# Summing the denominators of two pairs of key tiles in one visit instead of two

## What is computed

```python
q = (x1 @ wq.T).reshape(b, n, HEADS, HEAD_DIM).transpose(0, 2, 1, 3)
k = (x2 @ wk.T).reshape(b, m, HEADS, HEAD_DIM).transpose(0, 2, 1, 3)
v = (x2 @ wv.T).reshape(b, m, HEADS, HEAD_DIM).transpose(0, 2, 1, 3)
dots = jnp.einsum('bhnd,bhmd->bhnm', q, k) * SCALE
attn = jax.nn.softmax(dots, axis=-1)
out = jnp.einsum('bhnm,bhmd->bhnd', attn, v)
```

## Time and profile before

| | us |
|---|---|
| median of 3 runs | 1866.66 |
| lowest and highest | 1865.8, 1867.45 |
| the profiled execution | 1869.96 |
| its span, first to last instruction | 1867.9 |
| TensorE matmul busy | 1843.9 |
| VectorE busy | 1256.4 |
| ScalarE busy | 878.9 |
| GpSimd busy | 850.0 |
| VectorE: maxima (L1758), 1024 | 626.2 |
| VectorE: transposes of denominators (L1780), 78 | 55.6 |
| TensorE: denominators (L1448) | 98.7 |

### The profile page before, as it was taken

One profiled execution on the slowest core, in us unless ns is written; L12 is line 12 of the kernel. 1 busy time (PEld: TensorE's weight loads), 2 busy tenths in 40 slices (PEclk: granted clock), 3 DMA queues, 4 the chain that ended last, 5 costly groups with the idle time before them and its releaser, 6 DMA issues.

```text
span 1867.9 us, 27863 instructions
## 1 busy us (share of the span) xinstructions
PE 1843.9 (99%) x10488; PEld 1290.6 (69%) x10488; DVE 1256.4 (67%) x2339; ACT 878.9 (47%) x1587; POOL 850.0 (46%) x822
## 2 busy tenths in 40 slices
PE   9999999999999999999999999999999999999998
PEld 7786688788655555555555554554469998899986
DVE  6675574278787888888798799778554444344457
ACT  4322323322665666666465465457624443344433
POOL 4002201100598999998677577676122223222232
PEclk9999999999999999999999999999999999999999
DMA  8003535684767586858554443451244454534544
GB/s 289 24 1 118 186 103 178 199 243 144 170 139 168 130 202 130 176 112 178 109 135 114 103 118 87 112 115 63 79 148 127 132 142 107 141 91 131 145 111 155
DMA packets 124502, 250.19 MB, mean 134 GB/s; under 512 B 11312, under 2 KB 29504, under 8 KB 119680
## 3 DMA queue, kind: packets, MB, share of 16 engines
q1 hardware_dynamic: 109696, 187.56, 34.3%
q0 software_dynamic: 14672, 60.85, 16.0%
HBM read 148.46 MB, written 62.42 MB: 113 GB/s over the span
## 4 chain that ended last, share of the span: by engine, by line
PE 86%; DVE 9%; DMA 2%; issue 1%; POOL 1%; SPq 0%; ACT 0%; DVEq 0%; POOLq 0%; ACTq 0%
PE banks L1225 35%; PE banks L1540 12%; PE banks L1413 11%; PE banks L1424 11%; PE banks L1394 10%; DVE max L1758 5%; PE banks L1448 4%; PE banks L1231 2%; DMA raw<-in_x_t 1%; DVE den_t L1780 1%; PE banks L1325 1%; DMA k_half<-in_xwk_t 0%; DMA k_stack<-k_parts 0%; POOL x_nat L2297 0%; DVE hot_row L1936 0%
## 5 line engine op out<-in xcount | busy, mean ns | idle before, releaser
L2286 POOL TENSOR_TENSOR probs<-probs,probs 128x512 f32<-128x512 f32 x464 | 584.8, 1305 | 194.1 <-PE banks L1424 193.1
L2164 ACT ACTIVATE probs<-banks 128x512 f32<-128x512 f32 x1024 | 517.6, 626 | 286.9 <-PE banks L1413 286.4
L1758 DVE TENSOR_REDUCE max<-banks 128x1 f32<-128x512 f32 x1024 | 626.2, 680 | 37.4 <-PE banks L1394 37.0
L1413 PE MATMUL banks<-q_stack,k_stack 98*128 98x512 f32 x1024 | 403.3, 407 | 0.1
L1394 PE MATMUL banks<-k_stack,q_stack 98*128 98x512 f32 x1024 | 400.1, 398 | 1.4 <-DVE den_t L1780 1.1
L1413 PEld LDWEIGHTS banks<-q_stack,k_stack 98*128 98x128 f32 x1024 | 191.0, 187 | 151.7 <-issue 101.1
L1424 PE MATMUL banks<-probs,v_grp 128*32 128x512 f32 x2048 | 252.3, 605 | 0.0
L1394 PEld LDWEIGHTS banks<-k_stack,q_stack 98*128 98x128 f32 x1024 | 192.6, 188 | 48.5 <-DVE max L1758 13.5
L2344 POOL DMA_INDIRECT y_rows<-eo,tok x35 | 69.8, 1994 | 172.3 <-DVE eo L1991 116.2
L1424 PEld LDWEIGHTS banks<-probs,v_grp 128*32 128x32 f32 x2048 | 60.3, 110 | 118.3 <-issue 112.0
L1978 DVE TENSOR_TENSOR hid_lo<-hid,hid_hi 128x640 fp32r<-128x640 f32 x64 | 52.8, 824 | 126.3 <-ACT hid_hi L2233 126.3
(11 more groups left out here) (273 smaller groups left out, 2795.8 us busy)
## 6 DMA issues: line engine op xcount, KB each, us to landing
k_stack<-k_parts SPq DMA_DIRECT2D x144, 256.0 KB, 5.4
probs<-probs POOLq DMA_DIRECT2D x36, 1024.0 KB, 10.1
w_raw<-in_L_ffn_w SPq DMA_DIRECT2D x16, 2048.0 KB, 8.4
q_stack<-q_parts SPq DMA_DIRECT2D x48, 256.0 KB
v_grp<-v_rows SPq DMA_DIRECT2D x48, 256.0 KB, 3.5
raw<-in_ctx_t SPq DMA_DIRECT2D x8, 1024.0 KB, 6.6
k_parts<-out_hi SPq DMA_DIRECT2D x32, 256.0 KB, 2.5
k_parts<-out_lo SPq DMA_DIRECT2D x32, 256.0 KB, 3.2
```

Source lines behind the costliest of these rows:

```text
L1413: nc.tensor.matmul(out, keys_of(t)[0:STK + SHIFT, j, tile_of(s)], queries_of(t)[:, j, :], start=True, stop=True).then_inc(scored.sem, 1)
L1758: V.reduce_max(max4[:, tiles_of(t), :, :][:, k, j, mc:mc + 1], bank(bank_of["max", t, mc, k, j]), AX.X) \
L2164: S.activation(probs_of(t, s)[:, j, :], bank(bank_of["score", t, s, j]), ACT.Exp, scale=SCALE) \
L2286: G.tensor_tensor(a[:, j, :], a[:, j, :], b[:, j, :], ALU.add).then_inc(pair_added.sem, 1)
```

## The change

A pair that is the first of its four steps (s a multiple of 4), where pairs are summed and the turn is not the last, gets a due clock one later. The second pair of the four is due at that same clock, so both fall into one visit.

```diff
                     if not by_fours(turn, s):
-                        pending.append((clock + 1, turn, s + 1))
+                        pending.append((clock + (2 if s % FOUR == 0 and turn < LAST else 1), turn, s + 1))
                     elif s % FOUR == 2:
                         fours.append((turn, s + 1))
                         pending.append((clock + (3 if (turn, s // FOUR) in LAST_BEFORE_PLAIN else 4), turn, s + 1))
```

## The result

| | before | changed |
|---|---|---|
| median, us (4 runs each) | 1867.06 | 1885.36 |
| lowest and highest | 1865.8, 1869.21 | 1882.67, 1895.29 |
| ratio, 95% interval | | 1.0112 (1.0082 to 1.0142) |
| profiled execution, and its span | 1869.96, 1867.9 | 1882.67, 1880.9 |
| transposes of denominators (L1780) | 78 | 60 |

The medians alone give 1.0098, inside the interval. The profiled execution of the changed kernel is its fastest; its span is 13.0 us longer than that of the kernel before. The slowest, 1895.29, has a mean granted clock of 0.990 against 0.996.

The account below looks back on a forecast made before the run. TensorE, busy 1843.9 of 1867.9 us, was taken as the bound, with most transposes hidden. Terms +0.92 - 3.03 - 0.12 gave -2.2 us, from 1866.66 to 1864.5; own range 1861.8 to 1867.2, 8 in 10 1860.5 to 1868.3.

Parts of the forecast that it names:

- the sum over the 7 blocks and the 9 after them: Delayed blocks losing a visit and blocks after them: waits grow by 0.92 us in the former, 3.03 won in the latter.
- the blocks that get the second pair: TensorE reaches their scores 0.85 us later, VectorE catches up and delays go: -3.03 us in all.
- The 7 blocks that lose a visit: Blocks such as (11, 2), with a delay already: VectorE's lag grows and waits lengthen, +0.92 us in all.
- the 2.2 us: Whole kernel: the forecast gain, from +0.92 - 3.03 - 0.12 us.
- the 2.76 us in eight blocks: Delays in eight blocks that get the second pair, such as (9, 4) and (9, 12), expected to go: 2.76 us.
- Banks, taken as 0: Ring of banks: maxima wait for the fifth-last instead of the fourth-last, VectorE's pace decides as before; 0 us.
- The new wait: Merged visits wait for the second pair's additions on GpSimd; 0 us if the margin of 1.2 us holds.
- rival 2: Merged visits wait for GpSimd's additions: 0.3 us in each of 18 gives +5.4, so 1869.9 us; chance 0.08.
- Rival 1: VectorE's time counts in full in the 7 delayed blocks: 5.0 us beside the 2.2, so 1859.5 us; chance 0.15.
- TensorE's work: All 92 pairs and fours before the last turn still summed; -0.4 us, within the reading, taken as 0.
- Fewer than 55 cases: Sign expected in the trace: VectorE idle before a transpose less often than the 55 cases before.
- Rival 4: The clock drops once more in a delayed block: +3.4 - 2.2, so 1867.9 us; chance 0.05.

Follow-up runs that it names:

- e2: The changed kernel with GpSimd's pair additions of turns 8 to 14 cut from 512 to 32 columns; 1860.67 us, ratio 0.9967 to the kernel before.
- e1: The kernel before with GpSimd's pair additions of turns 8 to 14 cut from 512 to 32 columns; 1860.77 us, ratio 0.9965.
- e8: The changed kernel, with visits from turn 9 on taking their bank from the scores' ring; 1883.33 us, ratio 1.0082 to the kernel before.
- e7: The change made only in turn 10 and from step 8 of turn 12, 4 visits vanishing; 1866.86 us, ratio 0.9995 to the kernel before.

## Why the prediction was wrong

The forecast of 1864.5 and its range missed by far, 18.3 us slower against 2.2 faster, and the sign was wrong.

**The step that failed** is the sum over the 7 blocks and the 9 after them, and in it the term for the blocks that get the second pair. These nine were to grow by 0.85 us each less 3.03 of delays given back, 4.6 in all; they grew by 25.3, of which 3.4 are the clock's. The 7 blocks that lose a visit came out better than forecast, 7.0 us shorter against 5.2. The sum let VectorE's lag move from block to block with the length of its routing steps taken from the trace as a constant. That length isn't a constant: it was 0.17 us a step because of where GpSimd stood at that moment. The rows for this were at hand. Line 1905 already had both durations in the kernel before (shortest, median and longest of four, ns):

```profile
L1905 DVE TENSOR_TENSOR weight<-rt_ex,col_r x4: 166/197/1160, 981.1 to 1377.5; 128x8 f32<-128x8 f32 x4
```

And the pause of 1.38 us in the earlier trace rows was read only as a margin for GpSimd. The prediction moved TensorE's blocks by 0.87 us and did not ask what stood side by side afterwards on the two other engines. With the additions made small the step holds: e2's (9, 12) takes 7.46 us, where I had said 7.5, and the nine blocks are 4.4 us longer in e2 than in the kernel before, where I had said 4.6. But the medians of e1 and e2 are equal, so the 2.2 us vanish. A good part of the delays that they were to come from were meetings of the same sort, which e1 removes as well: of the 2.76 us in eight blocks it takes off 1.4.

**Banks, taken as 0**, was wrong as a place: a merged visit waits until an older maximum has freed its bank, and 16.1 us of TensorE's idle time ended there. e8 shows that another bank gives little of it back.

**The new wait.** The margin for GpSimd's additions held but for one place. The visit of (14, 8) waits 0.51 us for them:

```profile
1307.81 1.50 PE L1448 MATMUL banks<-probs,ones 128*32 128x512 f32 x12 [0.51 <-POOL probs L2286]
```

The margin of 1.2 us had been worked out for a short block of 5.72 us. In the second half of turn 14 the blocks have fewer maxima, and the short one before this visit takes 3.96. That is 0.5 of the 18 us: rival 2 had the right sign, but its mechanism isn't the one that cost the time.

**Rival 1**, that VectorE's time counts in full, is not what the change showed: VectorE's time rose. What a saved transpose is worth where no step is held up, no run shows by itself; e1 and e2, whose medians differ by 0.1 us, speak for next to nothing.

**What held.** TensorE's work didn't change: 5.72 became 5.75 without a visit, and a second pair costs 0.85 to 0.87. The counts of 60 transposes and 18 vanished visits are exact. Turn 10 and late turn 12 behaved as forecast, (9, 6) takes 5.74 us. In (11, 2) the block took 6.71 us with a lag of 1.93, against 7.0 and 2.3 forecast; the next block, (11, 4), took 2.1 us more than before. "Fewer than 55 cases" of idle time before a transpose was a poor test: 54.

**The clock** isn't the cause, but it adds to the loss. Within the loop the changed kernel has two drops, one in (9, 4) and one in (9, 12); the mean of these two stretches of 10 us is 0.83 each:

```profile
968.00:978.00 10.00, 8.47 (x44) 4.30 (x48) 8.12 (x14) 4.03 (x8) 4.22 (x6) 0.83 0.15 33
1002.00:1012.00 10.00, 8.20 (x44) 3.87 (x48) 8.13 (x16) 4.03 (x8) 2.58 (x3) 0.83 0.46 97
```

That is 3.4 us each at 1.2 GHz, so 3.4 us lost in all, as much as the kernel before loses at the table alone; there the changed kernel keeps 2.4 GHz. Each drop came at a long wait of TensorE: 3.70 us in (9, 12), and 2.61 in (9, 4). Two other waits of 2.61 us, in (11, 12) and (14, 4), came with no drop.

```profile
969.53 3.50 PE L1448 MATMUL banks<-probs,ones 128*32 128x512 f32 x16 [2.61 <-DVE max L1758]
```

Rival 4 thus happened, and in the profiled executions it was paid back elsewhere. Over all runs it wasn't: the changed kernel's four have granted clocks of 0.996, 0.995, 0.995 and 0.990, and 13 runs of the kernel before in the round of e1 have 0.996 to 0.998. By an estimate from these, some 3 of the median's 18.3 us are the clock's, set off by the waits.

## What to carry to other kernels

A plan's timing is shared by all engines: shortening one engine's block by under a microsecond can move another engine's small steps out of the pause of a third, and that price doesn't show in the rows of the block that is shortened. Before removing "hidden" work, look at what lies beside what on VectorE and GpSimd, and take the range of durations that one and the same small instruction shows in the trace as the warning. A merge that frees an engine which isn't the bound may be worth nothing, as in e7, and may still cost the rhythm.

## What the runs showed of the hardware

A VectorE instruction on 8 columns takes 0.17 us alone and 1.11 to 1.2 beside a chain of GpSimd additions of 512 columns, 0.58 to 0.65 beside additions of 256. It then ends within 0.05 us of the end of an addition. VectorE's maxima, which read a PSUM bank, aren't held up: the four of the earlier trace rows at 1090.59 take 2.44 us while the additions of the earlier trace rows run. Nor is a reduction in SBUF, as these instructions of the kernel before show, which run beside GpSimd's additions from 1286.93 to 1291.94: the reduction takes its 0.14 us, the addition next to it 1.16 where it takes 0.17 elsewhere.

```profile
1289.18 0.14 DVE L1903 TENSOR_REDUCE col_sum<-rt_ex 128x4 f32<-128x32 f32 x1
...
1289.57 1.16 DVE L1905 TENSOR_TENSOR weight<-rt_ex,col_r 128x8 f32<-128x8 f32 x1
```

It also goes the other way: GpSimd's addition of 16 columns (L2315), mostly 0.23 us, takes 2.18 at 1309.03, beside VectorE's pair addition of 2.25 us at 1308.87.

The Trainium skill ("SBUF — State Buffer", Who interferes with whom) says that VectorE and GpSimd share one pair of SBUF ports as an exclusive lock, held for a whole instruction; that an instruction of VectorE with two SBUF inputs contends for it with a GpSimd instruction that reads SBUF, and so can a copy, cast or scalar operation in a two-port mode; and that a reduction never does. The rows agree, though they don't show port modes: the instructions held up were tensor-tensor operations, casts, copies and scalar steps, and no reduction was. The rule bore on this change, and I didn't weigh it.

The meetings go on nearly one for one: in (9, 12) of the changed kernel four steps of VectorE, from 999.54 on, need three additions, so a chain of small steps advances by about one step per addition.
